# Four exact Q blocks in slots 8 to 61, one addition of O put ahead of the last reciprocal, and O's scales fetched one slot earlier

## The chip, the cores and the metric

The kernel runs on one core of a Trainium2 chip. Its engines are TensorE (PE in the profile; PEld is its weight load), VectorE (DVE), ScalarE (ACT), GpSimd (POOL) and SyncE (SP, which here only issues DMAs). The metric is the device time of one execution in microseconds. The kernel before takes 1048.83 us, the median of three runs (1047.40 to 1049.28).

## The reference, cut to what matters

One decoder layer in three parts, each behind a layer norm and added to `x` (2 batches, 512 tokens, 1024 wide):

```python
q = h @ dequant(q_codes, q_scales)      # 1024 -> 32 heads x 128; weights are (code - 8) * scale,
k = h @ dequant(k_codes, k_scales)      # one scale for 128 input rows and one output column
v = h @ dequant(v_codes, v_scales)      # k and v have 8 heads
q, k = rope(q), rope(k)
attn = softmax(q @ k.T / sqrt(128) + causal_mask)
x = x + (attn @ v) @ dequant(o_codes, o_scales)          # 4096 -> 1024
x = x + fake_quant(layernorm(x)) @ fake_quant(ctx)       # 1024 x 1024 for each batch
bw = mean(abs(w)) * sign(w) - clip(w) + clip(w)          # w is 1024 x 1024
x = x + layernorm(x) @ bw.T
```

## The kernel before, in words

**Precision.** Most products are made of two fp16 halves (hi and lo), so one 128-row block of a projection is three matmuls of 512 columns (`three_products`, L811 to L813). Codes minus 8 are exact in fp16. A block of Q that is multiplied by its exact codes needs two matmuls only (`q_exact`, L899: the two halves of the activations), and its scale is applied afterwards to what stands in PSUM: ScalarE multiplies the running sum by the ratio of this block's scale to the next one's (`q_base`, L1392). These blocks stand in a chain: matmul pair, ScalarE multiplies in place, next matmul pair. Of Q's 8 blocks `N_EXACT` = 4 are exact for slots in the range `MANY` and `FEW_EXACT` = 2 elsewhere.

**Slots.** After a first phase (layer norm, K and V, about 170 us) the attention runs in 64 slots, p = 0 to 63: one query head and one batch each. A slot's work is spread over all engines, and each engine's program is written out by hand, in one fixed order per engine; semaphores tie them together. In slot p TensorE makes scores of p in three units (L987), projects Q for slot p + 2, multiplies probabilities by V for p - 1 (`weigh`, L1003) and makes four units of the output projection O (`o_unit`, L1023). VectorE takes row maxima (`maxima`, L2236), adds O's units to the residual (`o_add`, 128 x 1024, L2249), sums the two rotary products (`q_sum`, L2144), and takes the reciprocals of the row sums: the first (three columns, L2323 or L2330), then the last (one column, L2338). ScalarE makes the exponentials (`exps`, L1425), copies, and high halves; GpSimd multiplies by the rotary tables (L1792, L1772), normalises the probabilities (L1777) and makes low halves (L1797, L1784). SyncE's queue issues the loads and the DMA transposes of the probabilities (`turn`, L726, four per slot), in written order, waiting where its next item is not ready.

**Two kinds of slots.** `many(p)` (p + 2 in `MANY`) picks the order within a slot. Before, it holds for p = 8 to 39. In such a slot TensorE's four exact pairs are spread between scores and O units; VectorE makes `q_sum` of the next slot before the third maxima and the first reciprocal; ScalarE makes `q_hi` and the O codes (`o_cut`) before the third exponential; and the half swap of the rotary input is made by two DMAs (`q_swap` on SyncE, L715). In the other slots `q_sum` comes after the first reciprocal, `q_hi` after the third exponential, and ScalarE makes the swap by two copies (L1300, L1301).

**Side work.** Slots 8 to 39 also quantise the context (ScalarE L1529, VectorE L2342). Slots 40 to 63 instead make the binarised weights of the last part, one 128 x 256 unit per slot: GpSimd clips (`wf_clip`, L1853), ScalarE takes the sign (`wf_sign`, L1487), VectorE the difference (`wf_difference`, L2196), GpSimd adds (`wf_add`, L1878), then, in the slot after, ScalarE makes the high half (`wf_upper`, L1494), VectorE the low half (`wf_lower`, L2202), and SyncE transposes both (L741). `wf_sign` of a unit waits for `wf_lower` of the one before it, which stands in the same slot, since both use one buffer:

```python
act.wait_ge(wf_clipped, u + 1)
if u >= 2:
    act.wait_ge(wf_split, u)        # wf_lower of unit u - 1
act.activation(diff, raw, ACT.Sign).then_inc(wf_signed, 1)
```

A piece of Q's weights is 128 x 512 codes. Where a whole piece is exact, in the even slots under `MANY`, ScalarE only converts the codes; else VectorE scales (`piece_scale`, L1984) and splits (`piece_lo`, L1990) and SyncE loads the scales (L625). `o_scales` (L1408) copies a head's O scales and its Q ratios from a table to `o_now`; the table's ratios are made in the first phase by `ratio_step`, one step in each of six pairs of K's loop.

## Time and profile before

| | |
|---|---|
| median of 3 runs | 1048.83 us |
| the profiled execution | 1048.89 us |
| its span | 1047.0 us |
| TensorE busy | 1009.6 us (96%), 5232 matmuls |
| VectorE, ScalarE, GpSimd busy | 903.0, 754.4, 774.2 us |
| granted TensorE clock | 0.998 of full (the 2.4 GHz level) |

The span is the time from the first to the last instruction; 1.9 us of the execution lie around it. The slices of the page show VectorE at nine tenths and GpSimd at nine tenths or more from about 630 us on, where the weights of the last part are made beside the attention, and GpSimd at seven or eight tenths before that. TensorE stands at nine tenths in nearly every slice, but its ends are modelled, so that a short wait between two matmuls does not show as idle time.

### The profile page before, as it was taken

What the parts mean: (1) busy time and instruction counts of PE and PEld (TensorE: products, weight loads), DVE (VectorE), ACT (ScalarE), POOL (GpSimd) and SP (SyncE); (2) the same over time, 40 slices, a digit from 0 to 9 for tenths busy, and PEclk for the clock granted to TensorE, in tenths of its full rate; (3) what the DMA queues carried; (4) which work ended last, traced back from release to release, by engine and by line L of the source; (5) the groups of instructions that cost most, each with busy time, mean ns of one, the idle gap of its engine ahead of it and who ended that gap; (6) DMA issues with size and microseconds to landing.
All of it is one profiled execution on the core that took longest, in us unless ns stands there. A gap on an engine that the chain in (4) does not pass through costs nothing.

```text
span 1047.0 us, 17502 instructions
## 1 busy us (share of the span) xinstructions
PE 1009.6 (96%) x5232; PEld 487.1 (47%) x5232; DVE 903.0 (86%) x1656; ACT 754.4 (72%) x1664; POOL 774.2 (74%) x833
## 2 busy tenths in 40 slices
PE   5999898999999999999999999999999999999998
PEld 3444343445544444444444444555555554454443
...
GB/s 337 255 196 129 96 46 22 145 155 153 165 181 175 173 177 173 172 181 173 180 174 171 177 182 141 160 157 152 152 155 157 156 139 114 111 122 84 85 103 81
DMA packets 312637, 158.53 MB, mean 151 GB/s; under 512 B 258496, under 2 KB 272960, under 8 KB 312544
## 3 DMA queue, kind: packets, MB, share of 16 engines
...
q14 instruction: 51, 0.42, 0.1%
...
## 4 chain that ended last, share of the span: by engine, by line
PE 62%; DVE 18%; issue 7%; ACT 7%; POOL 3%; DMA 1%; SPq 0%; ACTq 0%; DVEq 0%; POOLq 0%
PE proj_ps L1023 7%; PE side_ps L1003 7%; PE score_ps L987 6%; PE out_ps L1023 6%; DVE x_acc L2249 5%; PE side_ps L811 5%; PE side_ps L812 5%; PE side_ps L813 5%; PE proj_ps L1205 5%; PE side_ps L899 4%; PE proj_ps L1210 2%; PE score_ps L1175 2%; DVE score_ps L2236 2%; PE out_ps L834 1%; PE proj_ps L811 1%
## 5 line engine op out<-in xcount | busy, mean ns | idle before, releaser
L1777 POOL TENSOR_SCALAR prob<-prob,row_inv 128x512 f32<-128x512 f32 (+3 forms) x256 | 181.9, 721 | 86.3 <-DVE row_inv L2323 64.7
L1784 POOL TENSOR_TENSOR w_b<-prob,w_b 128x896 f16<-128x896 f32 (+2 forms) x192 | 185.9, 995 | 12.6 <-ACT w_b L1452 12.4
L2249 DVE SCALAR_TENSOR_TENSOR x_acc<-proj_ps,o_now,x_acc 128x1024 f32<-128x1024 f32 x120 | 153.0, 1275 | 6.1 <-PE proj_ps L1023 6.0
L2249 DVE SCALAR_TENSOR_TENSOR x_acc<-out_ps,o_now,x_acc 128x1024 f32<-128x1024 f32 x120 | 153.1, 1276 | 1.3 <-PE out_ps L1023 1.3
L1392 ACT ACTIVATE side_ps<-side_ps,o_now 128x512 f32<-128x512 f32 x184 | 121.4, 660 | 44.3 <-PE side_ps L899 42.2
L1425 ACT ACTIVATE prob<-score_ps,neg_max 128x512 f32<-128x512 f32 (+3 forms) x256 | 132.9, 522 | 26.1 <-DVE neg_max L2236 25.1
L987 PE MATMUL score_ps<-k_sb,q_sb 128*128 128x512 f16 (+3 forms) x768 | 141.1, 299 | 3.2 <-ACT prob L1425 2.1
L1023 PE MATMUL proj_ps<-work,w_b 128*128 128x512 f16 x496 | 137.9, 379 | 3.3 <-DVE x_acc L2249 1.5
L1023 PE MATMUL out_ps<-work,w_b 128*128 128x512 f16 x496 | 132.7, 379 | 1.1 <-DVE x_acc L2249 0.7
L2236 DVE CUSTOM_DVE_ANT_0 score_ps<-score_ps,mask_b 128x512 f32<-128x512 f32 (+3 forms) x256 | 122.4, 501 | 8.3 <-PE score_ps L987 8.3
L811 PE MATMUL side_ps<-hT,w_a 128*128 128x512 f16 x320 | 121.1, 379 | 0.7 <-ACT side_ps L1392 0.3
L813 PE MATMUL side_ps<-hT,w_a 128*128 128x512 f16 x320 | 121.2, 379 | 0.0
L812 PE MATMUL side_ps<-hT,w_a 128*128 128x512 f16 x320 | 121.2, 379 | 0.0
L1003 PE MATMUL side_ps<-work,v_sb 128*128 128x512 f16 (+3 forms) x768 | 116.4, 302 | 1.4 <-DMA work<-w_b 1.4
L899 PE MATMUL side_ps<-hT,w_a 128*128 128x512 f16 x368 | 109.5, 379 | 0.7 <-ACT side_ps L1392 0.6
L1452 ACT ACTIVATE w_b<-prob 128x896 f16<-128x896 f32 (+2 forms) x192 | 97.6, 550 | 11.9 <-POOL prob L1777 11.1
L987 PEld LDWEIGHTS score_ps<-k_sb,q_sb 128*128 128x128 f16 x768 | 71.8, 98 | 64.1 <-ACT prob L1425 5.5
L1772 POOL TENSOR_TENSOR swapped<-swapped,sin_t 128x512 f32<-128x512 f32 x77 | 99.6, 1294 | 0.0
L1003 PEld LDWEIGHTS side_ps<-work,v_sb 128*128 128x128 f16 x768 | 70.2, 99 | 47.2 <-DMA work<-w_b 2.3
L1797 POOL TENSOR_TENSOR q_sb<-rot,q_sb 128x512 f16<-128x512 f32 x62 | 79.6, 1284 | 0.0
L1792 POOL TENSOR_TENSOR rot<-stage_o,cos_t 128x512 f32<-128x512 f32 x60 | 76.4, 1273 | 0.0
L1023 PEld LDWEIGHTS out_ps<-work,w_b 128*128 128x128 f16 x496 | 47.0, 98 | 62.7 <-DVE x_acc L2249 8.1
...
## 6 DMA issues: line engine op xcount, KB each, us to landing
...
swapped<-stage_o SPq DMA_DIRECT2D x64, 128.0 KB, 2.3
...
```

What stands on the lines that cost most here:

```text
L811: pe.matmul(o, stat(0), mov(0), start=first, stop=False, skip_group_check=onto)
L812: pe.matmul(o, stat(0), mov(1), start=False, stop=False, skip_group_check=onto)
L813: return pe.matmul(o, stat(1), mov(0), start=False, stop=last, skip_group_check=onto)
L899: mm = pe.matmul(q_ps, w_a[:, 0, w:w + P], hT[:, l, e, i % B * S:(i % B + 1) * S], start=l + e == 0, stop=l == 1, skip_group_check=e > 0)
L987: mm = pe.matmul(o, q[n // 2], k[n % 2], start=n == 0, stop=n == 2)
L1003: mm = pe.matmul(pv_ps[:, kb * P:S], v_sb[:, bass.ds(g, 1), l, b * TB + kb, :].rearrange("p a d -> p (a d)"), probT[:, m, at:kb + (TB - 1) ...
L1023: mm = pe.matmul(o[:, b, :], o_codes[:, h % RING, cb * P:(cb + 1) * P], ao[:, h % 2, l, b * S:(b + 1) * S], start=l == 0, stop=l == 1)
L1425: ins = act.activation(prob[:, SCORE_AT[qb]:SCORE_AT[qb] + w], score_ps[:, score_bank(i, u), off:off + w], ACT.Exp, bias=neg_max[:, c:c + ...
L1777: return pool.tensor_scalar(prob[:, at:at + w], prob[:, at:at + w], row_inv[:, col:col + 1], P_UP, ALU.mult, ALU.mult)
L1784: ins = pool.tensor_tensor(prob16[:, 1, to:to + w], prob[:, at:at + w], prob16[:, 0, to:to + w], ALU.subtract)
L2236: ins = dve.tensor_tensor_reduce(s, s, mask_b[:, S - w:S], -1.0, MAX_FROM, ALU.add, ALU.min, neg_max[:, c:c + 1])
L2249: ins = dve.scalar_tensor_tensor(y, u, s, y, ALU.mult, ALU.add)
```

## The change

- `MANY` ends at 64 instead of 42: four exact blocks for slots 10 to 63, and so the order of `many(p)` in slots 8 to 61.
- In the slots of that order VectorE makes `o_add` of unit 1 between the first and the last reciprocal, and no longer after it.
- `o_scales`, which stood between the first two exponentials of an odd slot, stands at the end of the even slot ahead of it.
- The table of ratios is written in place by seven steps with fewer instructions; for this the Q scales are loaded rotated by three heads, in two DMAs.

```diff
--- before.py
+++ after.py
@@ -59,7 +59,7 @@
 Q_AHEAD = 2
 N_EXACT = 4
 FEW_EXACT = 2
-RATIO_STEPS = 6
+RATIO_STEPS = 7
 Q_LEAD = 3
 
 
@@ -193,7 +193,7 @@
 
 
 CTX_GROUPS = B * KB // 4
-MANY = range(SLOTS + Q_AHEAD, (CTX_GROUPS + 1) * SLOTS + Q_AHEAD)
+MANY = range(SLOTS + Q_AHEAD, N_SLOTS)
 
 
 def exact_of(p):
@@ -682,7 +682,8 @@
                 load_k(m)
             sp.wait_ge(h_landed[6 - TB], 32)
             sp.dma_start(scale_rows, scales[SCALE_ROW:SCALE_ROW + P, :]).then_inc(scale_rows_landed, 16)
-            sp.dma_start(q_scale_rows, q_scales).then_inc(scale_rows_landed, 16)
+            sp.dma_start(q_scale_rows[:, 0:(NH - Q_LEAD) * KB], q_scales[:, Q_LEAD * KB:NH * KB]).then_inc(scale_rows_landed, 16)
+            sp.dma_start(q_scale_rows[:, (NH - Q_LEAD) * KB:NH * KB], q_scales[:, 0:Q_LEAD * KB]).then_inc(scale_rows_landed, 16)
             sp.wait_ge(k_cut, 2 * NKV)
             for n in range(FIRST_PIECES):
                 if n >= 2:
@@ -876,7 +877,7 @@
 
             def turn_scales():
 
-                pe.wait_ge(scale_rows_landed, 32)
+                pe.wait_ge(scale_rows_landed, 48)
                 pe.wait_ge(h_ready, 2 * TB)
                 for c in range(UNITS):
                     mm = pe.transpose(pv_ps[:, c * P:(c + 1) * P], scale_rows[:, c * P:(c + 1) * P], ident[:, :])
@@ -1501,7 +1502,7 @@
                 has_piece = not (known(p) and p + FIRST_PIECES >= N_CUT)
 
                 next_q = (g, i + Q_AHEAD) if i < SLOTS - Q_AHEAD else (g + 1, i + Q_AHEAD - SLOTS)
-                if i % B and not many(p) and not (known(p) and p < O_LAG):
+                if i % B and not many(p - 1) and not (known(p) and p < O_LAG):
                     o_scales(g, i)
                 if with_ctx:
                     q, _ = ctx_half(g, i)
@@ -1514,8 +1515,6 @@
                 if many(p):
                     q_base(*next_q, 1)
                     exps(p, i, 0)
-                    if i % B:
-                        o_scales(g, i)
                     q_base(*next_q, 2)
                     exps(p, i, 1)
                     q_base(*next_q, 3)
@@ -1565,6 +1564,8 @@
                 prob_split(p, 1)
                 if known(p) and p == N_SLOTS - 1:
                     column_part(0, 0)
+                if many(p) and i % B == 0:
+                    o_scales(g, i + 1)
                 if not (known(p) and p < O_LAG):
                     ao_part(p - 1, (i - 1) % SLOTS)
 
@@ -2162,7 +2163,7 @@
                 if k:
                     dve.wait_ge(q_ratio_step, k)
                 else:
-                    dve.wait_ge(scale_rows_landed, 32)
+                    dve.wait_ge(scale_rows_landed, 48)
                 if k == 0:
                     ins = dve.tensor_tensor(by, of, of, ALU.mult)
                 elif k == 1:
@@ -2172,19 +2173,15 @@
                 elif k == 3:
                     ins = dve.reciprocal(per, by)
                 elif k == 4:
-                    dve.tensor_tensor(per[:, :, 0], rows[:, :, 0], per[:, :, 0], ALU.mult)
-                    ins = dve.tensor_tensor(per[:, :, 1:], by[:, :, 0:N_EXACT - 2], per[:, :, 1:], ALU.mult)
+                    dve.tensor_tensor(o_table[:, :, CB], rows[:, :, 0], per[:, :, 0], ALU.mult)
+                    dve.tensor_tensor(o_table[:, :, CB + 1:CB + N_EXACT - 1], by[:, :, 0:N_EXACT - 2], per[:, :, 1:], ALU.mult)
+                    ins = dve.tensor_scalar(o_table[:, :, CB + N_EXACT - 1], by[:, :, N_EXACT - 2], Q_UP, None, ALU.mult)
+                elif k == 5:
+                    c = FEW_EXACT - 1
+                    for r0, r1 in ((0, MANY[0] // B - Q_LEAD), ((MANY[-1] + 1) // B - Q_LEAD, NH)):
+                        ins = dve.tensor_scalar(o_table[:, r0:r1, CB + c], by[:, r0:r1, c - 1], Q_UP, None, ALU.mult)
                 else:
-                    h0, h1 = MANY[0] // B, (MANY[-1] + 1) // B
-                    for c, row, up in [(e, per[:, :, e], 1.0) for e in range(N_EXACT - 1)] + [
-                            (N_EXACT - 1, by[:, :, N_EXACT - 2], Q_UP)]:
-                        dve.tensor_scalar(o_table[:, h0 - Q_LEAD:h1 - Q_LEAD, CB + c], row[:, h0:h1], up, None, ALU.mult)
-                    for c, row, up in [(e, per[:, :, e], 1.0) for e in range(FEW_EXACT - 1)] + [
-                            (FEW_EXACT - 1, by[:, :, FEW_EXACT - 2], Q_UP)]:
-                        dve.tensor_scalar(o_table[:, 0:h0 - Q_LEAD, CB + c], row[:, Q_LEAD:h0], up, None, ALU.mult)
-                        if h1 < NH:
-                            dve.tensor_scalar(o_table[:, h1 - Q_LEAD:NH - Q_LEAD, CB + c], row[:, h1:NH], up, None, ALU.mult)
-                        ins = dve.tensor_scalar(o_now[:, 1, CB + c:CB + c + 1], row[:, Q_LEAD - 1:Q_LEAD], up, None, ALU.mult)
+                    ins = dve.tensor_copy(o_now[:, 1, CB:CB + N_EXACT], o_table[:, NH - 1, CB:CB + N_EXACT])
                 ins.then_inc(q_ratio_step, 1)
 
             def wf_difference(u):
@@ -2334,6 +2331,8 @@
                     (late_join, late_sum, late_lower)[p]()
                 if has_piece and not whole(n):
                     piece_scale(n, i % 2, exact)
+                if many(p):
+                    o_add(p, i, 1)
                 dve.wait_ge(exp_done, p * 3 + 3)
                 dve.reciprocal(row_inv[:, 3:4], row_sum[:, 3:4]).then_inc(inv_ready[1], 1)
                 if with_ctx:
@@ -2347,7 +2346,8 @@
                 if known(p) and wf_early(p) is not None:
                     wf_difference(wf_early(p))
                 if has_o:
-                    o_add(p, i, 1)
+                    if not many(p):
+                        o_add(p, i, 1)
                     o_add(p, i, 2)
                 if known(p) and 0 < p < O_LAG:
                     v_rest(V_HERE + p - 1)
```

VectorE in slot 44, from the end of the maxima to the last addition of O; `x_acc<-out_ps` is an odd unit of O, `x_acc<-proj_ps` an even one, `rot<-rot,swapped` is `q_sum`, `w_b<-w_b` is `wf_lower` and `w_b<-w_b,wf_mean` is `wf_difference`. Before:

```order
L2236 ISA score_ps,neg_max<-score_ps,mask_b 128x256
L2236 ISA neg_max 128x1
L2249 SCALAR_TENSOR_TENSOR x_acc<-proj_ps,o_now,x_acc 128x1024
L2330 RECIPROCAL row_inv<-row_sum 128x3
L2144 TENSOR_TENSOR rot<-rot,swapped 128x512
L1984 SCALAR_TENSOR_TENSOR stage_s<-stage_c,stage_s 128x256
L2338 RECIPROCAL row_inv<-row_sum 128x1
L2202 SCALAR_TENSOR_TENSOR w_b<-w_b 128x256
L1990 SCALAR_TENSOR_TENSOR w_a<-stage_s,w_a 128x256
L2196 SCALAR_TENSOR_TENSOR w_b<-w_b,wf_mean 128x256
L2249 SCALAR_TENSOR_TENSOR x_acc<-out_ps,o_now,x_acc 128x1024
```

And now:

```order
L2246 SCALAR_TENSOR_TENSOR x_acc<-proj_ps,o_now,x_acc 128x1024
L2145 TENSOR_TENSOR rot<-rot,swapped 128x512
L2233 ISA score_ps,neg_max<-score_ps,mask_b 128x256
L2233 ISA neg_max 128x1
L2320 RECIPROCAL row_inv<-row_sum 128x3
L2246 SCALAR_TENSOR_TENSOR x_acc<-out_ps,o_now,x_acc 128x1024
L2337 RECIPROCAL row_inv<-row_sum 128x1
L2199 SCALAR_TENSOR_TENSOR w_b<-w_b 128x256
L2193 SCALAR_TENSOR_TENSOR w_b<-w_b,wf_mean 128x256
L2246 SCALAR_TENSOR_TENSOR x_acc<-proj_ps,o_now,x_acc 128x1024
```

`q_sum` has moved ahead of the maxima and the first reciprocal, the odd unit's addition ahead of the last reciprocal, and the two operations on the piece are gone in this even slot.

ScalarE in slot 47, an odd one, from the second exponential on; `q_sb<-rot` is `q_hi`, `w_b<-stage_o` is `o_cut`, the L1494 row is `wf_upper`, the L1487 row `wf_sign`, `stage_o<-side_ps` is `q_copy`, `w_b<-prob` are the high halves of the probabilities. Before:

```order
L1438 ACTIVATE w_b<-stage_o 128x512
L1425 ACTIVATE prob,row_sum<-score_ps,neg_max 128x384
L1425 ACTIVATE prob,row_sum<-score_ps,neg_max 128x128
L1494 ACTIVATE w_b<-w_b 128x256
L1425 ACTIVATE prob,row_sum<-score_ps,neg_max 128x256
L1400 ACTIVATE q_sb<-rot 128x512
L1295 ACTIVATE w_a<-stage_s 128x512
L1487 ACTIVATE w_b<-w_b 128x256
L1382 ACTIVATE stage_o<-side_ps 128x512
L1452 ACTIVATE w_b<-prob 128x896
L1300 ACTIVATE swapped<-stage_o 64x512
L1301 ACTIVATE swapped<-stage_o 64x512
```

And now:

```order
L1426 ACTIVATE prob,row_sum<-score_ps,neg_max 128x128
L1393 ACTIVATE side_ps<-side_ps,o_now 128x512
L1401 ACTIVATE q_sb<-rot 128x512
L1439 ACTIVATE w_b<-stage_o 128x512
L1495 ACTIVATE w_b<-w_b 128x256
L1426 ACTIVATE prob,row_sum<-score_ps,neg_max 128x256
L1296 ACTIVATE w_a<-stage_s 128x512
L1488 ACTIVATE w_b<-w_b 128x256
L1383 ACTIVATE stage_o<-side_ps 128x512
L1453 ACTIVATE w_b<-prob 128x896
```

`q_hi`, `o_cut` and `wf_upper` now stand between `q_sum` and the third exponential, and the two swap copies are gone.

SyncE over one slot of this stretch, from one load of O's codes to the next. Before:

```order
L631 DMA stage_o<-in_codes_dram 128x512
L726 DMA_TRANSPOSE work<-w_b 128x7x128
L726 DMA_TRANSPOSE work<-w_b 128x5x128
L726 DMA_TRANSPOSE work<-w_b 128x7x128
L726 DMA_TRANSPOSE work<-w_b 128x5x128
L621 DMA stage_c<-in_codes_dram 128x512
L625 DMA stage_s<-in_scales_dram 128x256
L734 DMA w_b<-in_ffn_w_dram 128x256
L741 DMA_TRANSPOSE k_sb<-w_b 128x2x128
L741 DMA_TRANSPOSE v_sb<-w_b 128x2x128
```

And now:

```order
L631 DMA stage_o<-in_codes_dram 128x512
L716 DMA swapped<-stage_o 64x512 x2
L727 DMA_TRANSPOSE work<-w_b 128x7x128
L727 DMA_TRANSPOSE work<-w_b 128x5x128
L727 DMA_TRANSPOSE work<-w_b 128x7x128
L727 DMA_TRANSPOSE work<-w_b 128x5x128
L621 DMA stage_c<-in_codes_dram 128x512
L735 DMA w_b<-in_ffn_w_dram 128x256
L742 DMA_TRANSPOSE k_sb<-w_b 128x2x128
L742 DMA_TRANSPOSE v_sb<-w_b 128x2x128
```

Two swap DMAs have come in front of the four transposes of the probabilities, and the load of scales is gone where the piece is whole.

## Rows read from the trace of the kernel before

**Rows 1.** The page: shares of the chain that ended last; landing of the swap.

```profile
PE 62%; DVE 18%; issue 7%; ACT 7%; POOL 3%; DMA 1%; SPq 0%; ACTq 0%; DVEq 0%; POOLq 0%
...
swapped<-stage_o SPq DMA_DIRECT2D x64, 128.0 KB, 2.3
```

**Rows 2.** Windows between last reciprocals: slots 40-61, one pair of each kind.

```profile
core 0: us, PE busy (x) PEld busy (x) DVE busy (x) ACT busy (x) POOL busy (x), PEclk, DMA share, GB/s
...
633.17:873.54 240.37, 240.37 (x1302) 121.94 (x1301) 231.94 (x417) 203.24 (x482) 226.93 (x253) 1.00 0.71 151
498.67:521.25 22.58, 22.46 (x122) 10.80 (x120) 19.22 (x36) 19.07 (x44) 18.18 (x21) 1.00 0.76 175
679.03:701.95 22.92, 22.92 (x126) 11.62 (x125) 22.37 (x41) 19.42 (x47) 21.74 (x25) 1.00 0.75 156
```

**Rows 3.** Timeline, slots 29 and 30, VectorE: start us, us, instruction [idle before].

```profile
508.40 0.17 DVE L2323 RECIPROCAL row_inv<-row_sum 128x3 f32<-128x3 f32 x1
...
517.71 1.28 DVE L2249 SCALAR_TENSOR_TENSOR x_acc<-proj_ps,o_now,x_acc 128x1024 f32<-128x1024 f32 x1
518.90 0.68 DVE L2144 TENSOR_TENSOR rot<-rot,swapped 128x512 f32<-128x512 f32 x1
...
519.84 0.17 DVE L2323 RECIPROCAL row_inv<-row_sum 128x3 f32<-128x3 f32 x1
521.25 0.16 DVE L2338 RECIPROCAL row_inv<-row_sum 128x1 f32<-128x1 f32 x1 [1.24 <-ACT prob L1425]
```

**Rows 4.** Timeline, slot 30, TensorE and ScalarE.

```profile
519.04 0.60 PE L1023 MATMUL proj_ps<-work,w_b 128*128 128x512 f16 x2
...
519.62 0.63 ACT L1400 ACTIVATE q_sb<-rot 128x512 f16<-128x512 f32 x1 [0.16 <-DVE rot L2144]
...
520.67 0.46 ACT L1425 ACTIVATE prob<-score_ps,neg_max 128x256 f32<-128x256 f32 x1
```

**Rows 5.** Timeline, slots 29 and 30, GpSimd.

```profile
510.24 1.16 POOL L1797 TENSOR_TENSOR q_sb<-rot,q_sb 128x512 f16<-128x512 f32 x1
...
512.86 2.90 POOL L1784 TENSOR_TENSOR w_b<-prob,w_b 128x896 f16<-128x896 f32 x3
...
516.96 1.27 POOL L1772 TENSOR_TENSOR swapped<-swapped,sin_t 128x512 f32<-128x512 f32 x1
...
521.40 1.16 POOL L1797 TENSOR_TENSOR q_sb<-rot,q_sb 128x512 f16<-128x512 f32 x1
...
523.90 1.89 POOL L1784 TENSOR_TENSOR w_b<-prob,w_b 128x896 f16<-128x896 f32 x1 [0.36 <-ACT w_b L1452]
```

**Rows 6.** Timeline, slots 44 and 45, GpSimd.

```profile
680.28 1.32 POOL L1797 TENSOR_TENSOR q_sb<-rot,q_sb 128x512 f16<-128x512 f32 x1
...
685.41 0.72 POOL L1878 TENSOR_TENSOR w_b<-w_b 128x256 f32<-128x256 f32 x1
...
688.56 0.40 POOL L1853 TENSOR_SCALAR w_b<-w_b 128x256 f32<-128x256 f32 x1
689.83 2.21 POOL L1777 TENSOR_SCALAR prob<-prob,row_inv 128x512 f32<-128x512 f32 x2 [0.86 <-DVE row_inv L2330]
```

**Rows 7.** Timeline, slots 44 and 45, VectorE and ScalarE.

```profile
679.10 0.76 DVE L2202 SCALAR_TENSOR_TENSOR w_b<-w_b 128x256 f16<-128x256 f32 x1
680.51 1.38 DVE L2196 SCALAR_TENSOR_TENSOR w_b<-w_b,wf_mean 128x256 f32<-128x256 f32 x1
...
691.54 1.04 DVE L1990 SCALAR_TENSOR_TENSOR w_a<-stage_s,w_a 128x512 f16<-128x512 f32 x1
...
680.75 0.94 ACT L1452 ACTIVATE w_b<-prob 128x896 f16<-128x896 f32 x1
...
688.65 0.42 ACT L1494 ACTIVATE w_b<-w_b 128x256 f16<-128x256 f32 x1
```

**Rows 8.** Timeline, SyncE's queue: a swap of slot 29, the transposes of slot 44.

```profile
511.51 1.11 SPq L715 DMA_DIRECT2D swapped<-stage_o  x2
...
683.65 5.20 SPq L726 DMA_TRANSPOSE work<-w_b  x4
```

**Rows 9.** VectorE by line and form, 90 to 175 us: count, busy us, mean ns.

```profile
L2181 DVE TENSOR_SCALAR work<-ctx_raw 128x16 f32<-128x16 f32 x4 | 1.5, 439 | 0.0
```

## The prediction

> **What bounds the kernel now.** I read the chain of waits first: TensorE holds 62% of it and VectorE 18% [rows 1], so TensorE is the bound on the whole, but not which loop sets a slot's period. The windows between two last reciprocals tell that. A pair of slots (even and odd alternate exactly) lasts 22.58 us where the order of `many` holds and 22.92 us in slots 40 to 61 [rows 2]. In the second TensorE is busy throughout, and no matmul starts late: its 88 matmuls of 512 columns and 12 each of 384, 256 and 128 columns are 54,272 columns, 0.4223 ns each, or 0.216 us for one of 512 columns. A `many` pair has four matmuls of 512 columns less: 22.92 - 4 x 0.216 = 22.06 us. It lasts 22.58, so TensorE loses 0.52 us there. The busy column (22.46 of 22.58) hides most of this loss, since matmul ends are modelled. In the timeline the even slot shows it: the fifth O matmul group starts at 519.04 [rows 4], just when `o_add` of unit 0 ends at 517.71 + 1.28 = 518.99 [rows 3]. VectorE is late there, while it has sat idle for 1.24 us before the last reciprocal of the same kind of slot, waiting for ScalarE's exponential [rows 3].
>
> In slots 40 to 61 the second engine is GpSimd: 21.74 us busy of 22.92, against 18.18 in a `many` pair [rows 2]. The weights of the last part add 0.72 us (`wf_add`) and 0.40 us (`wf_clip`) to each slot [rows 6].
>
> **The change, part by part.**
>
> *Slots 8 to 39, the earlier addition.* In an even slot the addition (1.2 us from start to start) now fills the idle 1.24 us; in an odd slot `piece_scale` and it (0.66 + 1.2) put the last reciprocal some 0.45 us later, but what follows it, the context's operation, waits for ScalarE anyway. So VectorE enters the next slot 1.2 us earlier, more than TensorE's waits for it. I take nearly all of the 0.52 us per pair as gained: -0.5. From slot 8 to 39 there are 16 pairs, and the last is mixed: 15.4 x 0.5 = -7.7 us. Bounds: 0 (another wait takes its place) and 16 x 0.52 = -8.3 us. The port is no obstacle: `o_add` reads PSUM and one SBUF operand. The Trainium skill (SBUF — State Buffer, Who interferes with whom) says that a VectorE instruction with at most one SBUF input, outside the 2-port modes, does not contend with GpSimd; the sum would be the same without this sentence.
>
> *`o_scales` one slot earlier.* One copy of 12 columns on ScalarE, moved to where it waits for the V product anyway. 0, bounds -0.2 and +0.2 us per pair.
>
> *Ratio table.* The twelve instructions of the last two steps, four of them 1.5 us together [rows 9], become six in three steps; the Q scales' second DMA has tens of us to land. I take -0.5 us, bounds -1.3 and +0.5.
>
> *Slots 40 to 61, the matmuls.* 44 matmuls less, 44 x 0.216 = 9.5 us of TensorE. This is gained only if TensorE stays the bound. So I walk round the loop that the new order closes: first reciprocal of p -> GpSimd's normalising, `q_lo`, low halves, `wf_add`, both rotary products -> `q_sum` -> third maxima -> first reciprocal of p + 1. Before, `q_sum` came behind the reciprocal, so this loop was open there; in slots 8 to 39 it is closed, but without the weights' work. Times are counted from the first reciprocal.
>
> 1. From GpSimd's low halves to the end of the sine product: 516.96 + 1.27 - 512.86 = 5.37 us [rows 5].
> 2. `wf_add` in between: +0.70 (0.72 less the overlap) [rows 6].
> 3. From the end of the sine to the next first reciprocal. GpSimd goes straight on to `wf_clip`, +0.40 less 0.03; `q_sum` has two SBUF operands and is held until it ends. Held instructions are seen in the trace: `wf_difference` took 1.38 us and ended 0.29 us behind `q_lo` (680.51 + 1.38 against 680.28 + 1.32), `piece_lo` of 512 columns took 1.04 and ended 0.54 behind the normalising (692.58 against 689.83 + 2.21) [rows 6, 7]. So `q_sum` ends 0.37 + 0.54 = 0.91 behind the sine, and the reciprocal starts 519.84 - (518.90 + 0.68) = 0.26 later [rows 3]: 1.2 with the signal.
> 4. From the reciprocal to the low halves. Without hindrance this is 523.90 - 519.84 = 4.06 in an even slot (0.36 of it waiting for ScalarE) and 512.86 - 508.40 = 4.46 in an odd one [rows 3, 5]. Here a longer way opens. ScalarE now makes `wf_upper` (0.42) ahead of the third exponential, which otherwise starts at 0.83: the last reciprocal comes at 0.83 + 0.42 + 0.58 = 1.83 at the earliest [rows 3, 4, 7], in odd slots at about 1.86 behind the moved addition. `wf_lower`, next on VectorE, would start at 1.9. But GpSimd's `q_lo` starts at 1.56 (even) and 1.84 (odd) and ends at 2.72 and 3.00 [rows 5]. `wf_lower` reads two SBUF operands and is held until then: it ends at 3.01 and 3.29. Behind it wait `wf_sign`, `q_copy` and the first high halves, in this order on ScalarE; from the end of `wf_lower` to the end of these halves the trace has 681.69 - 679.86 = 1.83 us [rows 7]. With 0.06 for the signal, GpSimd's low halves start at 4.90 (even) and 5.18 (odd).
>
> A loop is then 4.90 + 5.37 + 0.70 + 1.20 = 12.17 us in even slots and 12.45 in odd ones, a pair 24.6 instead of 22.92. The slots 41 to 60 give 10 pairs: 246.2 us; slot 40 has no `wf_lower`: 4.06 + 7.27 = 11.3. Together 257.5 against 240.4 [rows 2]: +17.1. TensorE is up to some 1.2 us ahead of this loop when it closes (the addition came earlier by that much), which is absorbed once: +15.9 us. Bounds: -9.5 (TensorE alone) and +22 (each slot 0.3 later).
>
> The port is what makes items 3 and 4. The Trainium skill (SBUF — State Buffer, Who interferes with whom) calls it an exclusive lock, held for the whole instruction, against a GpSimd instruction that reads SBUF, and says that issue order decides who blocks. The trace agrees with 1.38 us for `wf_difference`. By that rule a pair comes to 24.6 us; if the two shared the bandwidth instead, it would come to about the 23.0 of the second rival.
>
> *The swap by DMA in slots 40 to 61.* ScalarE is freed of two copies that nobody will miss. SyncE's queue gets 1.16 us per slot (1.11 and a gap) [rows 8] behind the weights' second transpose, which waits for `wf_lower`: 3.05 + 1.24 + 0.63 + 1.16 = 6.1, landed 2.3 us later [rows 1] at 8.4; the sine starts at 4.90 + 0.70 + 5.37 - 1.27 = 9.7. Covered by 1.3 us. The four transposes of the probabilities (5.20 us) [rows 8] end at 11.4 instead of some 10.8 and still land ahead of the V product.
>
> *Pieces.* `piece_scale` and `piece_lo` of even slots go (about 0.9 us of VectorE per pair); VectorE isn't last in the loop. 0.
>
> **Sum.** The profiled execution took 1048.89 us, 0.06 over the median: 1048.9 - 7.7 - 0.5 + 15.9 = 1056.6.
>
> **The rivals.**
>
> *TensorE stays the bound to the end.* For it: it is the bound in both stretches now. Against it: it needs a loop under 11.03 us per slot, and items 1 to 3 (7.27 us) leave 2 x 3.76 = 7.5 us of a pair for item 4, which needs 3.70 + 4.46 = 8.2 even without any wait for ScalarE. Slots 40 to 61 would last 22.06 to 22.5 per pair: -9.5 to -4.6, with the rest 1031 to 1036 us. Faster.
>
> *The loop closes, but without the detour over `wf_lower`*, because `wf_lower` slips in ahead of `q_lo` and delays it by 0.16 to 0.3 only. Then 4.06 - 0.36 + 0.16 = 3.86 and 4.46 + 0.16 = 4.62 give slots of 11.13 and 11.89 us, a pair 23.0: +1 us there, 1042 us in all. Faster. For it: in odd slots the two starts are only 0.1 us apart. Against it: in even slots they are 0.3 apart.
>
> *A half way:* held in even slots, slipped in in odd ones, 0.56 less per pair than forecast: 1056.6 - 5.6 = 1051.0, or about 1049 if one more tenth per slot is saved. Near no change.
>
> *SyncE's queue.* It gets 1.16 us more per slot beside 5.20 us of transposes. If the swap lands more than 1.3 us later than usual, behind the weights' transposes, the sine waits for it: each 0.3 us beyond that is 6 us over 20 slots, 1060 to 1066. Slower. The same range holds if slots 8 to 39 gain nothing.
>
> *That the change doesn't do what it says* would show as a matmul count other than 5232 - 44; the order of instructions leaves no room for it.
>
> **How the numbers follow.** Forecast (both slots held, 1050 to 1060) 0.57; TensorE bound 0.12; loop without the detour 0.18; half way 0.08; queue or no early gain 0.05. A measurement of this kernel can tell about 0.2%, 2 us, from no change. Faster: 0.12 + 0.18 = 0.30 and a part of the half way, 0.31; within 0.2%: 0.07; slower: 0.62. The time is the likeliest case's, rounded to 1056. The range leaves out the TensorE case's lower part and the queue's upper: 1036 to 1062; the likeliest case's own is 1050 to 1060. The sign hangs on item 4.
>
> **What would show it.** Right: last reciprocals of slots 8 to 39 come 22.1 us apart per pair; of slots 41 to 60 over 24 us apart; there TensorE shows idle time, `wf_lower` takes about 1.1 us and ends 0.3 behind `q_lo`; GpSimd waits about 1 us for ScalarE's L1453 ahead of the low halves, and `q_sum` waits for the sine. Wrong: TensorE still busy throughout in slots 40 to 61, or pairs there under 23 us, or `wf_lower` at 0.4 to 0.8 us; or slots 8 to 39 unchanged, which would say that VectorE's lateness was not what TensorE waited for.

## The result, and the profile after

The changed kernel takes 1057.37 us (median of 4 runs, 1056.54 to 1058.56) against 1048.29 for the kernel before in the same comparison (4 runs, 1047.40 to 1049.28): ratio 1.0087, 95% interval 1.0070 to 1.0105. It is slower by 9 us; 1056 was forecast, with a range of 1036 to 1062. The profiled execution took 1056.54 us with a span of 1054.7; it is the fastest of the four, so that the two profiles lie 7.7 us apart where the medians lie 9.1.

The page of the kernel after, its busy times and the shares of the chain that ended last:

```profile
PE 999.9 (95%) x5178; PEld 478.6 (45%) x5188; DVE 895.2 (85%) x1628; ACT 743.0 (70%) x1653; POOL 761.6 (72%) x833
...
PE 56%; POOL 13%; DVE 13%; ACT 8%; issue 8%; DMA 1%; ACTq 0%; SPq 0%; DVEq 0%; POOLq 0%
```

TensorE has fewer matmuls (5188 weight loads are 5232 - 44; the matmul count misses ten records) and a smaller share of the chain, 56% instead of 62% [rows 1]. GpSimd's share went from 3% to 13%: the last chain now runs through it.

Windows of the kernel after, between last reciprocals: slots 8 to 39, slots 40 to 60, one pair of each kind (columns as in [rows 2]):

```profile
272.33:626.21 353.88, 353.88 (x1921) 174.85 (x1920) 311.48 (x577) 302.61 (x689) 291.53 (x322) 1.00 0.82 178
626.21:882.37 256.16, 239.25 (x1266) 112.95 (x1265) 219.26 (x397) 195.07 (x472) 215.26 (x254) 1.00 0.74 158
504.59:526.71 22.12, 22.12 (x121) 10.92 (x120) 19.47 (x37) 18.92 (x44) 18.20 (x21) 1.00 0.80 177
676.44:700.97 24.53, 22.79 (x122) 10.68 (x121) 21.05 (x38) 18.57 (x47) 20.50 (x25) 1.00 0.78 158
```

The first and third line are the gain: a pair of slots fell from 22.58 to 22.12 us, and slots 8 to 39 from 360.28 (272.89 to 633.17) to 353.88, by 6.40. The second and fourth are the loss: the pair rose from 22.92 [rows 2] to 24.53, the stretch from 240.37 to 256.16, by 15.79, and TensorE, always busy there before, is busy 22.79 of 24.53. Ahead of slot 8 the kernel gained 0.56 us (272.33 against 272.89), behind slot 61 1.13. Together -0.56 - 6.40 + 15.79 - 1.13 = +7.7, the difference of the spans, 1054.7 and 1047.0.

The timeline of the kernel after shows the closed loop. GpSimd, slots 46 and 47 (it answers to [rows 6]):

```profile
699.09 1.16 POOL L1798 TENSOR_TENSOR q_sb<-rot,q_sb 128x512 f16<-128x512 f32 x1
700.23 1.00 POOL L1778 TENSOR_SCALAR prob<-prob,row_inv 128x128 f32<-128x128 f32 x2
702.45 2.90 POOL L1785 TENSOR_TENSOR w_b<-prob,w_b 128x896 f16<-128x896 f32 x3 [1.22 <-ACT w_b L1453]
705.31 0.73 POOL L1879 TENSOR_TENSOR w_b<-w_b 128x256 f32<-128x256 f32 x1
705.99 1.28 POOL L1793 TENSOR_TENSOR rot<-stage_o,cos_t 128x512 f32<-128x512 f32 x1
707.21 1.28 POOL L1773 TENSOR_TENSOR swapped<-swapped,sin_t 128x512 f32<-128x512 f32 x1
708.46 0.41 POOL L1854 TENSOR_SCALAR w_b<-w_b 128x256 f32<-128x256 f32 x1
710.00 1.53 POOL L1778 TENSOR_SCALAR prob<-prob,row_inv 128x512 f32<-128x512 f32 x2 [1.14 <-DVE row_inv L2320]
711.50 1.15 POOL L1798 TENSOR_TENSOR q_sb<-rot,q_sb 128x512 f16<-128x512 f32 x1
...
714.85 2.90 POOL L1785 TENSOR_TENSOR w_b<-prob,w_b 128x896 f16<-128x896 f32 x3 [0.54 <-ACT w_b L1453]
```

VectorE in the same slots (it answers to [rows 7]):

```profile
699.25 0.16 DVE L2337 RECIPROCAL row_inv<-row_sum 128x1 f32<-128x1 f32 x1 [0.37 <-ACT prob L1426]
699.33 1.20 DVE L2199 SCALAR_TENSOR_TENSOR w_b<-w_b 128x256 f16<-128x256 f32 x1
...
708.52 0.88 DVE L2145 TENSOR_TENSOR rot<-rot,swapped 128x512 f32<-128x512 f32 x1 [0.51 <-POOL swapped L1773]
709.33 0.42 DVE L2233 CUSTOM_DVE_ANT_0 score_ps<-score_ps,mask_b 128x256 f32<-128x256 f32 x1
709.67 0.13 DVE L2233 DVE_READ_ACCUMULATOR2_ANT neg_max<- 128x1 f32 x1
709.67 0.16 DVE L2320 RECIPROCAL row_inv<-row_sum 128x3 f32<-128x3 f32 x1
...
711.53 0.15 DVE L2337 RECIPROCAL row_inv<-row_sum 128x1 f32<-128x1 f32 x1
711.60 1.33 DVE L2199 SCALAR_TENSOR_TENSOR w_b<-w_b 128x256 f16<-128x256 f32 x1
```

And ScalarE between them:

```profile
700.63 0.42 ACT L1488 ACTIVATE w_b<-w_b 128x256 f32<-128x256 f32 x1 [0.89 <-DVE w_b L2199]
700.95 0.58 ACT L1383 ACTIVATE stage_o<-side_ps 128x512 f32<-128x512 f32 x1
701.43 1.45 ACT L1453 ACTIVATE w_b<-prob 128x896 f16<-128x896 f32 x3
```

Follow it: GpSimd's sine (L1773) frees `q_sum` (L2145), which frees the first reciprocal (L2320), which frees GpSimd's normalising and `q_lo` (L1798). `wf_lower` (L2199) is held behind `q_lo`, 1.20 us in place of the 0.4 us seen below; `wf_sign` (L1488) waits for it, `q_copy` and the high halves (L1453) stand behind `wf_sign`, and GpSimd waits 1.22 us for them before its low halves (L1785), from which the sine comes again. The way from `q_lo` over `wf_lower`, `wf_sign` and the high halves to the low halves is called the detour below.

### The profile page after: what moved, and what is told of

Read it like the earlier page. It is cut to its first block, busy times and chain, and to the rows that moved or that the text cites. A ratio compares the mean times of both kernels' runs of the same rounds, so it can differ in the third digit from the quotient of the medians.

```text
span 1054.7 us, 17443 instructions
## 1 busy us (share of the span) xinstructions
PE 999.9 (95%) x5178; PEld 478.6 (45%) x5188; DVE 895.2 (85%) x1628; ACT 743.0 (70%) x1653; POOL 761.6 (72%) x833
## 4 chain that ended last, share of the span: by engine, by line
PE 56%; POOL 13%; DVE 13%; ACT 8%; issue 8%; DMA 1%; ACTq 0%; SPq 0%; DVEq 0%; POOLq 0%
PE out_ps L1024 6%; PE proj_ps L1024 6%; PE side_ps L1004 6%; PE side_ps L900 6%; PE score_ps L988 6%; PE side_ps L812 4%; PE side_ps L813 4%; PE side_ps L814 4%; PE proj_ps L1206 4%; POOL w_b L1785 4%; POOL swapped L1773 3%; POOL rot L1793 3%; DVE w_b L2199 2%; PE score_ps L1176 2%; PE proj_ps L1211 2%
## 5 line engine op out<-in xcount | busy, mean ns | idle before, releaser
L1778 POOL TENSOR_SCALAR prob<-prob,row_inv 128x512 f32<-128x512 f32 (+3 forms) x256 | 175.3, 697 | 89.3 <-DVE row_inv L2320 83.2
L1785 POOL TENSOR_TENSOR w_b<-prob,w_b 128x896 f16<-128x896 f32 (+2 forms) x192 | 185.7, 995 | 30.1 <-ACT w_b L1453 30.0
L1393 ACT ACTIVATE side_ps<-side_ps,o_now 128x512 f32<-128x512 f32 x228 | 150.6, 661 | 56.8 <-PE side_ps L900 56.8
L988 PE MATMUL score_ps<-k_sb,q_sb 128*128 128x512 f16 (+3 forms) x768 | 144.5, 299 | 3.3 <-ACT prob L1426 2.1
L900 PE MATMUL side_ps<-hT,w_a 128*128 128x512 f16 x456 | 135.8, 379 | 12.3 <-ACT side_ps L1393 10.6
L1024 PE MATMUL proj_ps<-work,w_b 128*128 128x512 f16 x496 | 144.9, 379 | 2.2 <-DVE x_acc L2246 1.5
L1024 PE MATMUL out_ps<-work,w_b 128*128 128x512 f16 x496 | 136.1, 379 | 1.2 <-DVE x_acc L2246 0.7
L812 PE MATMUL side_ps<-hT,w_a 128*128 128x512 f16 x276 | 104.4, 378 | 0.5 <-ACT side_ps L1393 0.3
L814 PE MATMUL side_ps<-hT,w_a 128*128 128x512 f16 x276 | 104.5, 379 | 0.0
L813 PE MATMUL side_ps<-hT,w_a 128*128 128x512 f16 x276 | 104.5, 379 | 0.0
L1453 ACT ACTIVATE w_b<-prob 128x896 f16<-128x896 f32 (+2 forms) x192 | 95.1, 549 | 11.1 <-POOL prob L1778 10.9
L1773 POOL TENSOR_TENSOR swapped<-swapped,sin_t 128x512 f32<-128x512 f32 x77 | 99.9, 1297 | 0.0
L2262 DVE SCALAR_TENSOR_TENSOR work<-side_ps,work 128x512 f16<-128x512 f32 x64 | 44.2, 691 | 42.2 <-ACT work L1462 42.2
```

Of the source, the lines that this page charges most:

```text
L812: pe.matmul(o, stat(0), mov(0), start=first, stop=False, skip_group_check=onto)
L813: pe.matmul(o, stat(0), mov(1), start=False, stop=False, skip_group_check=onto)
L814: return pe.matmul(o, stat(1), mov(0), start=False, stop=last, skip_group_check=onto)
L900: mm = pe.matmul(q_ps, w_a[:, 0, w:w + P], hT[:, l, e, i % B * S:(i % B + 1) * S], start=l + e == 0, stop=l == 1, skip_group_check=e > 0)
L988: mm = pe.matmul(o, q[n // 2], k[n % 2], start=n == 0, stop=n == 2)
L1024: mm = pe.matmul(o[:, b, :], o_codes[:, h % RING, cb * P:(cb + 1) * P], ao[:, h % 2, l, b * S:(b + 1) * S], start=l == 0, stop=l == 1)
```

## The experiments

Each ratio is to the kernel before on the same chip, with its 95% interval; that kernel took 1048.29 us beside the kernel after, 1047.47 beside e1 to e4, 1047.51 beside e5 to e8, 1047.59 beside e9, e9b and e10, and 1047.25 beside e11, so that times of different rows compare to about 1 us. A pair is the time from a last reciprocal to the one after the next, in slots 42 to 59.

| run | what it is | us | ratio | pair |
|---|---|---|---|---|
| before | | 1048.29 | 1 | 22.92 |
| after | | 1057.37 | 1.0087 (1.0070-1.0105) | 24.53 |
| e1 | old range, early addition | 1039.62 | 0.9926 (0.9913-0.9939) | 22.92 |
| e2 | long range, late addition | 1057.90 | 1.0099 (1.0086-1.0112) | 23.97 |
| e3 | second difference buffer | 1048.22 | 1.0005 (0.9994-1.0015) | 23.7 |
| e4 | `q_sum` behind the reciprocal | 1048.95 | 1.0014 (1.0005-1.0022) | 23.6 |
| e5 | `wf_clip` behind `q_lo` | 1058.39 | 1.0098 (1.0085-1.0112) | 24.55 |
| e6 | a block of Q less | 1056.70 | 1.0084 (1.0070-1.0098) | 24.53 |
| e7 | e4, swap by ScalarE | 1084.76 | 1.0352 (1.0337-1.0368) | 27.1 |
| e8 | e7, addition behind | 1048.57 | 1.0005 (0.9996-1.0014) | 23.73 |
| e9 | e8, swap between blocks | 1043.81 | 0.9960 (0.9946-0.9975) | 23.37 |
| e9b | e9, one difference buffer | 1044.67 | 0.9970 (0.9958-0.9981) | 23.37 |
| e10 | `q_lo` one later | 1046.14 | 0.9985 (0.9976-0.9994) | 23.6 |
| e11 | e1 with three exact blocks | 1059.38 | 1.0113 (1.0096-1.0129) | 24.70 |

The pairs of e3, e4, e7 and e10 are twice a mean, since their slots are uneven; e6's is that of its regular slots.

### The two halves of the change

**e1**, everything but the longer range:

```diff
-MANY = range(SLOTS + Q_AHEAD, N_SLOTS)
+MANY = range(SLOTS + Q_AHEAD, (CTX_GROUPS + 1) * SLOTS + Q_AHEAD)
```

> The changed kernel with MANY ending at 42 again, so that only the earlier addition, the earlier copy of O's scales and the shorter ratio table are left. Theory (slots 8 to 39 gained 6.4 us because VectorE's lateness was what TensorE waited for, slots 40 to 61 lost 15.8 us through the longer range): 1041 us, pairs in slots 8 to 39 of 22.1 us, in 40 to 61 of 22.9 as before. Rival (the gain in slots 8 to 39 is only a shift of when the reciprocal stands in its slot, given back later): 1048 us.

Measured: 1039.62 us, 7.9 less than before on that chip (1047.47), and faster than both kernels. Its windows between last reciprocals, slots 8 to 39 and 40 to 60:

```profile
272.47:625.38 352.91, 352.91 (x1918) 174.71 (x1916) 311.22 (x578) 301.08 (x687) 290.93 (x321) 1.00 0.82 179
625.38:865.74 240.36, 240.36 (x1302) 121.93 (x1301) 231.92 (x417) 203.16 (x482) 226.91 (x253) 1.00 0.71 151
```

360.28 - 352.91 = 7.37 us are gained in the first, and the second is what it was before, 240.37 [rows 2]. So the whole loss is the longer range's. The gain can be read from who waits for whom. Between 280 and 600 us of the kernel before, TensorE's weight loads for O wait for VectorE's addition (us in all, times, the longest):

```profile
PEld out_ps L1023 <- DVE x_acc L2249: 5.6, 14, 0.4
PEld proj_ps L1023 <- DVE x_acc L2249: 5.6, 14, 0.4
```

e2, which has the late addition again, has the same two waits, 5.6 us each; the kernel after and e1 have none. The earlier copy of O's scales came and went together with the addition in both runs, so its own part in the 7.37 us is not measured; no such wait names it.

**e2**, the longer range with `o_add` of unit 1 and `o_scales` at their old places:

```diff
-                if many(p):
-                    o_add(p, i, 1)
                 dve.wait_ge(exp_done, p * 3 + 3)
...
-                    if not many(p):
-                        o_add(p, i, 1)
+                    o_add(p, i, 1)
                     o_add(p, i, 2)
```

> The changed kernel with the longer MANY, but the addition of O's unit 1 behind the last reciprocal and O's scales between the exponentials, as before. Theory: slots 8 to 39 at 22.58 us per pair again, slots 40 to 61 at about 24.5, since the loop through GpSimd does not hold this addition: 1048.3 - 0.5 + 15.9 = 1064 us. In the odd slots the last reciprocal comes 0.15 us earlier without the addition ahead of it, and the low half of the weights could then start just ahead of q_lo (it started 0.1 us behind it): then these slots are some 0.6 us shorter, 1058 us. Rival (the earlier addition is what costs in slots 40 to 61): 1048 us or less.

Measured: 1057.90 us, the lower of the two figures. The odd slot tells why. VectorE of e2, an even and an odd slot:

```profile
680.75 1.20 DVE L2199 SCALAR_TENSOR_TENSOR w_b<-w_b 128x256 f16<-128x256 f32 x1
...
692.80 0.16 DVE L2335 RECIPROCAL row_inv<-row_sum 128x1 f32<-128x1 f32 x1 [0.97 <-ACT prob L1426]
692.88 0.40 DVE L2199 SCALAR_TENSOR_TENSOR w_b<-w_b 128x256 f16<-128x256 f32 x1
```

and GpSimd's `q_lo` there:

```profile
680.51 1.16 POOL L1798 TENSOR_TENSOR q_sb<-rot,q_sb 128x512 f16<-128x512 f32 x1
...
692.93 1.38 POOL L1798 TENSOR_TENSOR q_sb<-rot,q_sb 128x512 f16<-128x512 f32 x1
```

In the even slot `q_lo` starts 0.24 us ahead of `wf_lower`, which then takes 1.20 us. In the odd slot `wf_lower` starts 0.05 us ahead of `q_lo`: it takes 0.40, and `q_lo` grows from 1.16 to 1.38. The pair is 23.97 us instead of 24.53. The kernel after has one such slot itself, its slot 60: `wf_lower` at 871.06 takes 0.41 us, `q_lo` starts at 871.11, and the next last reciprocal comes 11.39 us later instead of 12.28. In e5 `wf_lower` of slot 60 is held and that slot takes 12.13 us, so some 0.74 us of the difference is the hold and the rest belongs to the slot.

### Which parts of the loop count

**e3** gives odd units of the weights a second buffer for their difference, so that `wf_sign` no longer waits for the `wf_lower` just ahead of it:

```diff
+            if u > KB and u % 2:
+                return wf_words[:, WF_W:2 * WF_W], ctx_raw[:, 0:WF_W]
...
-                    act.wait_ge(wf_split, u)
+                    act.wait_ge(wf_split, u - 1 if u > KB else u)
```

> The changed kernel with a second buffer for the difference of the weights from slot 41 on, so that ScalarE's sign no longer waits for VectorE's low half in the same slot. Theory (the detour q_lo, held low half, sign, copy of Q, first high halves costs 1.0 us in even and 0.5 us in odd slots): pairs of 23.1 to 23.4 instead of 24.5 us, 1044 to 1047 us. Rival 1 (SyncE's queue sets the period of slots 40 to 61): no change, 1057 us. Rival 2 (the chain of exact blocks between TensorE and ScalarE sets it): no change either.

Measured: 1048.22 us, 9 less than the kernel after but above the 1047 of the expectation. So the wait of `wf_sign` for `wf_lower`, a link of the detour, carried about half of the rise of the pair, 0.8 of 1.61 us. The slots now take between 11.3 and 13.0 us with no steady pattern; of the chain of this run SyncE's queue holds 14% (0% in the kernel after), to which e4 below comes back.

**e10** leaves all buffers alone and moves one instruction: in slots 41 to 61 GpSimd does `norm(0)` first and `q_lo` behind it.

```diff
+                    if lo_later:
+                        norm(0)
                     if not (known(p) and p >= N_SLOTS - 1) and by_parts(p + 1):
                         q_lo(p + 1)
-                    norm(0)
+                    if not lo_later:
+                        norm(0)
```

> The changed kernel with one thing moved: from slot 41 on GpSimd makes q_lo (1.16 us, two SBUF operands) behind the normalising of the 128 columns instead of ahead of it. Nothing is added or removed. Theory (VectorE's low half of the weights is held until q_lo ends, and sign, copy of Q, high halves and GpSimd's low halves follow it): the low half is now held by the short normalising only and ends 0.6 to 0.7 us earlier, 0.6 us less in each of 20 slots: 1057.4 - 12 = 1045 us, bounds 1041 and 1050. Rival (the lost time does not run through this hold): 1057 us, or more since q_lo is later for TensorE's scores.

Measured: 1046.14 us, 11.2 below the kernel after (10.5 when each is taken against its own kernel before). VectorE of e10, an even and an odd slot:

```profile
673.31 0.41 DVE L2203 SCALAR_TENSOR_TENSOR w_b<-w_b 128x256 f16<-128x256 f32 x1
...
684.78 0.40 DVE L2203 SCALAR_TENSOR_TENSOR w_b<-w_b 128x256 f16<-128x256 f32 x1
```

GpSimd's `q_lo` starts at 673.41 and 685.31, behind both. The hold is gone, though every instruction is still there. Between 640 and 860 us `wf_sign` waits 2.0 us in all for `wf_lower` instead of 17.3, GpSimd's low halves wait 2.6 us for the high halves instead of 15.8, and the pair falls by about 0.9 us. The pair had risen by 1.61 us, so the hold of `wf_lower` made more than half of the loss, and it hangs on which of two instructions on two engines starts first.

**e4** opens the loop itself: `q_sum` goes behind the first reciprocal and `q_hi` behind the third exponential in slots 40 to 61.

```diff
                     o_add(p, i, 0)
-                    q_sum(p + 1)
+                    if not opened(p):
+                        q_sum(p + 1)
...
                     dve.reciprocal(row_inv[:, 0:3], row_sum[:, 0:3]).then_inc(inv_ready[0], 1)
+                    if opened(p):
+                        q_sum(p + 1)
```

> The changed kernel with q_sum behind the first reciprocal and q_hi behind the third exponential in slots 40 to 61, as those slots had it before; four exact blocks, the swap by DMA and TensorE's order stay. Theory (what costs is the loop reciprocal, GpSimd, q_sum, reciprocal, which is open now; and the last reciprocal comes early enough for the low half to start ahead of q_lo): pairs of 22.1 to 22.9 us, 1033 to 1042 us. Rival (SyncE's queue): 1057 us if it is the bound now, or a pair of some 22.7 to 23 if it is next. Rival 2 (exact blocks): 1057 us.

Measured: 1048.95 us, a miss. The chain of waits of e4 over two slots, shares by line:

```profile
by line: SPq L731 21.1%; issue 13.5%; SPq L746 9.7%; ACT prob L1430 5.3%; DVE w_b L2206 5.1%; DVE x_acc L2253 4.8%; SPq L720 4.3%; PE side_ps L904 4.2%; ACT w_b L1457 4.1%; SPq L625 4.0%; SPq L739 3.4%; PE score_ps L992 2.6%; ACT q_sb L1405
```

SyncE's queue, which had 0% of the chain of both kernels, is named first: it issues the transposes of the probabilities (L731), those of the weights (L746) and the swap (L720). But in this window the chain is followed back from an instruction of the queue itself; in the chain of the whole run the queue holds 9%. Another row of e4 speaks for a second cause. Its longest wait between 640 and 860 us is:

```profile
ACT w_b L1492 <- DVE w_b L2206: 29.2, 18, 1.9
```

So `wf_sign` waits for `wf_lower` more than in the kernel after (17.3 us): `wf_lower` is still held in both kinds of slots (1.33 and 1.25 us), against the second half of the expectation. With `q_sum` out of the loop the detour still closes over GpSimd's own order: its `q_lo` of 672.61 and the one of 695.99 lie 23.38 us apart, and in between it waits 0.22 us for a reciprocal and 1.22 and 0.54 us for the high halves of the detour. e4 doesn't part the two causes.

For the queue speaks e10, whose whole chain is:

```profile
PE 58%; SPq 17%; DVE 7%; POOL 7%; issue 4%; ACT 4%; DMA 2%; ACTq 0%; DVEq 0%; POOLq 0%
```

In e10 the same queue has a single line of waits between 640 and 860 us:

```profile
SPq L742 <- ACT w_b L1495: 0.6, 2, 0.3
```

It is 0.6 us of waiting in 220: the queue issues nearly all the time. In the kernel after it waited 9.2 + 4.7 us there, in the one before 20.7 + 0.8. TensorE's weight loads for the V product wait 13.8 us for the landing of transposes in e10, 9.0 in the kernel after. So at 11.6 to 11.8 us a slot the queue, which got the swap's 1.12 us, is the next bound by the chain of e10. No run took its load away from e10 alone, so what that would give is not shown.

**e5** puts `wf_clip` behind `q_lo`, so that `q_sum` isn't held by it:

```diff
-                    if known(p) and wf_early(p) is not None:
+                    if known(p) and wf_early(p) is not None and not clip_late:
                         wf_clip(wf_early(p))
...
                         q_lo(p + 1)
+                    if clip_late:
+                        wf_clip(wf_early(p))
```

> The changed kernel with GpSimd's clip of the weights behind q_lo instead of behind the sine in slots 41 to 62. There GpSimd waits 1.2 us for ScalarE ahead of the low halves in even slots, so that the clip is free. Theory: q_sum is no longer held by the clip and ends 0.72 us behind the sine instead of 0.91, 0.19 us less for each of 20 slots: 1057.4 - 3.8 = 1053.6 us. Rival (the loop does not run through q_sum): 1057.4 us, or more where the clip delays the normalising.

Measured: 1058.39 us, a miss: nothing gained. In its waits, 640 to 860 us, `wf_sign` now waits for the clip (L1854):

```profile
ACT w_b L1488 <- POOL w_b L1854: 20.7, 17, 1.4
```

`q_sum` takes 0.69 us again instead of 0.88, as expected. But the clip came off one piece of the loop and onto another, the detour, where it costs as much: `wf_sign` starts 0.58 us behind the end of `q_lo` instead of 0.38. The expectation took the clip as free there and left out that `wf_sign` waits for it.

**e6** takes load from TensorE. In slots 40 to 61 it leaves block 6 of Q out of the computation, so that the attention's result is wrong by it and each slot has three matmuls of 512 columns less:

```diff
-                    q_part(*ahead, range(N_EXACT, KB))
+                    q_part(*ahead, (4, 5, 7) if known(p) and p >= WF_FROM else range(N_EXACT, KB))
```

> The changed kernel with one of the four unscaled-code blocks of Q left out of the product in slots 40 to 61 (the result of the attention is that without this block): three matmuls of 512 columns, 0.65 us of TensorE, less per slot. Theory (TensorE waits for the loop there): 1057 us, within 1 us of the changed kernel. Rival (TensorE, or its chain with ScalarE, sets the period): 22 x 0.65 = 14 us less, 1043 us.

Measured: 1056.70 us with the same slots of 12.26 and 12.28 (two of them are longer, 12.84 and 12.62). A window of the length of a pair (columns as before):

```profile
675.00:699.50 24.50, 21.39 (x114) 9.83 (x113) 21.02 (x39) 18.54 (x46) 20.46 (x25) 1.00 0.71 158
```

TensorE is busy 21.39 us instead of 22.1 to 22.8 in two such windows of the kernel after, and the period stays. TensorE doesn't set it.

### Can the longer range be had at all?

**e7** is e4 with the swap made by two copies on ScalarE again, in place of the DMA, to relieve the queue:

```diff
-                    if many(p):
+                    if many(p) and not opened(p):
                         q_swap(p + Q_AHEAD)
```

> e4 (q_sum behind the first reciprocal from slot 40) with the swap made by ScalarE again in slots 40 to 61, so that SyncE's queue has two DMAs (1.16 us) less per slot. In e4 the queue ran without a pause in these slots, 23.4 us and more per pair. Theory (e4 missed its expectation because the queue became the bound): pairs of 22.1 to 22.9 us, 1036 to 1044 us against 1049. Rival (something else bounds e4: the held low half of even slots): 1049 us, since ScalarE only gets more to do.

Measured: 1084.76 us, the largest miss. Its waits, 640 to 860 us:

```profile
PEld side_ps L905 <- ACT side_ps L1398: 41.9, 41, 2.5
DVE work L2270 <- ACT work L1467: 33.7, 16, 2.2
...
ACT w_b L1493 <- DVE w_b L2207: 27.9, 17, 1.9
```

The copies stand in ScalarE's order ahead of the base of the next exact block, for which TensorE waits (first line). The scores come late, `q_sum` and `o_add` of unit 1 stand ahead of the last reciprocal, `wf_lower` is late and held, and `wf_sign`, `q_copy` and the copies wait for it: another closed loop, through ScalarE and TensorE. The run can't tell whether the relieved queue would have helped. Its granted TensorE clock was 0.986 to 0.992 in the four executions (in the profiled one 0.93 from 688 to 711.4 us, where TensorE often waits), against 0.994 or more in all other runs; how much of the loss that is was not measured.

**e8** takes `o_add` of unit 1 out of that path in slots 40 to 61 (behind the last reciprocal, as before the change):

```diff
-                if many(p):
+                if many(p) and not opened(p):
                     o_add(p, i, 1)
```

> e7 with O's unit 1 added behind the last reciprocal in slots 40 to 61, as before there (ahead of it in slots 8 to 39). In e7 the last reciprocal waits for q_sum and this addition, so that the low half of the weights comes late. Theory: pairs of 22.1 to 22.6 us, TensorE busy throughout again, 1031 to 1038 us, under the 1039.6 of e1. Rival (GpSimd's and VectorE's load bounds such a pair at the 22.9 us it had before): 1039 to 1041 us.

Measured: 1048.57 us: 36 less than e7 by one addition moved, so that addition was in e7's loop, but a miss by over 10 us.

**e9** also moves the two copies into the next slot, between the bases of the exact blocks, and has e3's buffer:

```diff
                     q_base(*next_q, 1)
+                    if behind:
+                        q_swap_half(p + 1, 1)
                     exps(p, i, 0)
```

> e8 with ScalarE's two swap copies moved into the next slot, one behind each of its first two exact blocks, and with e3's second buffer. In e8 the swap stood between the high halves and the copy of the V product, ahead of the first exact block of the next slot, which TensorE waits for. Theory (a second loop: Q's product, its copy, high halves, swap, V copy, exact block, TensorE): 1.26 us less in that loop, pairs of 22.1 to 22.9 us, 1031 to 1040 us. Rival (ScalarE, some 10.9 us busy per slot, is the bound by its load): 1044 to 1048 us.

**e9b** is e9 without e3's buffer:

> e9 without the second buffer, so that the sign of the weights again waits for the low half. Theory (in this order the last reciprocal is early and the low half is not held by q_lo): within 2 us of e9. Rival (the wait for the low half still stands in the loop): 5 us or more above e9.

Measured: 1043.81 and 1044.67 us. Slots of 11.67 and 11.70, even and steady, where TensorE idles 0.17 to 0.28 us and ScalarE 0.84 to 1.36. e9 is a miss too, 3.8 us above the forecast and just under the 1044 to 1048 of the rival, but the rival's reason, ScalarE full by its load, doesn't fit its idle time. With `wf_lower` hardly held (0.41 and 0.76 us in e9b), the second buffer gives 0.9 us, within the 2 us, and none of it in the pairs, which are the same.

**e11** goes another way: e1's order with three exact blocks instead of two in slots 42 to 63.

```diff
+LATE_EXACT = 3
...
+                if three:
+                    q_exact(*ahead, 2)
+                    o_unit(p, i, 1)
...
+                        q_base(*next_q, 2)
```

> e1 (MANY to 42, the earlier addition) with three exact blocks instead of two for the Q products of slots 42 to 63, in the old order of slots 40 to 61: q_sum stays behind the first reciprocal, the swap on ScalarE. The third block stands behind the third scores on TensorE, with O's unit 1 in front of the rest of Q's product to cover ScalarE's 0.66 us. 22 matmuls of 512 columns less, 22 x 0.216 = 4.7 us. Theory (what cost in the change is the order that came with the four blocks, not the exact blocks): TensorE stays the bound or nearly so, 22.5 us per pair, 1035 us, up to 1038 where VectorE (22.4 us busy of a 22.9 us pair) or GpSimd (21.7) takes over part. Rival (exact blocks cost ScalarE more than they save TensorE in these slots): 1040 us or more.

Measured: 1059.38 us, a miss on the side of the rival named there. ScalarE of e11:

```profile
709.82 0.66 ACT L1401 ACTIVATE side_ps<-side_ps,o_now 128x512 f32<-128x512 f32 x1
...
714.05 0.60 ACT L1391 ACTIVATE stage_o<-side_ps 128x512 f32<-128x512 f32 x1 [1.14 <-PE side_ps L818]
```

and TensorE, which starts Q's last blocks when the first of these is done:

```profile
710.62 0.38 PE L816 MATMUL side_ps<-hT,w_a 128*128 128x512 f16 x1 [0.78 <-ACT side_ps L1401]
```

The base of block 2 stands behind the second exponential, Q's last matmuls wait for it, and `q_copy` (L1391) with all behind it waits for them. At this place the third exact block takes a matmul from TensorE and puts 0.66 us of ScalarE in the path; other places for it were not tried.

## Why the prediction was right

**What bounds.** Right: in slots 8 to 39 TensorE lost about half a microsecond per pair to VectorE's late addition, and in slots 40 to 61 it stopped being the bound (e6).

**Slots 8 to 39.** -0.5 per pair and -7.7 in all were said; a pair fell by 22.58 - 22.12 = 0.46, the stretch by 6.40 in the kernel after and 7.37 in e1. The 1 us between these two lies at the seam: the last reciprocals of slots 37 to 40 come 10.73, 11.39 and 9.53 us apart in e1, 10.54, 11.58 and 10.55 in the kernel after.

**The ratio table.** -0.5 was said, and slot 8 came 0.56 earlier, but not because the instructions got cheaper. VectorE of the kernel after, by line and form, 90 to 175 us (it answers to [rows 9]):

```profile
L2184 DVE COPY o_now<-work 128x4 f32<-128x4 f32 x1 | 1.2, 1232 | 0.0
L2182 DVE TENSOR_SCALAR work<-ctx_raw 128x2 f32<-128x2 f32 x1 | 1.2, 1231 | 0.0
```

Two small writes alone take 2.5 us, where the four of [rows 9] took 1.5 together. Where the 0.56 comes from is open: here the figure was right by luck. The 1.13 us gained behind slot 61 were not foreseen.

**The loop, item by item.** Items 1 and 2, from the low halves to the end of the sine: 5.37 + 0.70 = 6.07 was said, 707.21 + 1.28 - 702.45 = 6.04 measured. Item 3, `q_sum` held by the clip: 1.20 said; the reciprocal comes at 709.67, 1.18 behind the sine's end, and `q_sum` takes 0.88 us instead of 0.68 [rows 3]. Item 4, the detour in the odd slot: low halves 5.18 behind the first reciprocal was said, 714.85 - 709.67 = 5.18 measured; `wf_lower` ends 0.28 behind `q_lo` in both slots. The loop is 722.08 - 709.67 = 12.41 us (said: 12.45) and in even slots 24.53 - 12.41 = 12.12 (12.17). GpSimd waits 1.22 and 0.54 for the high halves; "about 1" was said of both.

The rule of the Trainium skill (SBUF — State Buffer, Who interferes with whom), an exclusive lock whose holder is set by issue order, fits these rows, and e2 and e10 show its other half: the same instruction takes 0.40 us when it starts first, 0.05 and 0.10 us ahead of `q_lo`.

**The sum of slots 40 to 61.** +15.9 was said, +15.79 measured, in part by parts that cancel, so that the closeness is luck: slot 40 took 11.71 us instead of 11.3, the 1.2 us of TensorE's lead are not to be seen as a step of their own, the pairs came 0.1 shorter than 24.6, and slot 60 took 11.39 where 12.17 was said, since `wf_lower` slipped in there. The whole, +7.7 said and +7.7 between the two profiled executions, is as close by the same luck; the medians differ by 9.1.

**The rivals.** That TensorE stays the bound: refuted by the idle time and by e6. The loop without the detour is what e10 made, at 11.49 and 11.70 us a slot at best, 23.2 a pair where 11.13 and 11.89, a pair of 23.0, were said; on the mean its pair is 23.6, and the prediction had no term for the rest, for which e10's chain names SyncE's queue. The half way is e2's order, and the 0.56 us less per pair that were said of it are what e2 shows, 24.53 - 23.97. SyncE's queue did not bind in the kernel after: the swap is issued by 702.48 + 1.12 = 703.60 and lands 2.9 to 3.3 us behind its issue (2.3 was said), at 706.9 at the latest; the sine starts at 707.21, with no wait for it. It comes into the chain one step further down: 0% in the kernel after, 9% in e4, 14% in e3, 17% in e10.

**What stays open.** Whether slots 40 to 61 can run under 22.92 us a pair with more than two exact blocks. The best here is e9 with 23.37. The best whole kernel is e1.
